# Two layers on one core: the low-rank weights of the second layer leave the experts' loop

## The chip, the cores and the metric

The kernel runs on one core of one Trainium2 chip, as one program. The metric is the device time of one execution in microseconds; each kernel is executed several times and the median is compared. All tensors are 32-bit floats. The core has five engines that run their own instruction streams and meet at semaphores: TensorE (PE), VectorE (DVE), ScalarE (ACT), GpSimd (POOL) and SyncE (SP), which here only issues DMAs. GpSimd issues the gathers (indirect DMAs).

## The reference, cut to what matters

```python
x = hidden_states                                  # 8 x 256 tokens, 512 features
xn = layernorm(x)
x = x + L0_attn(xn) + L0_ffn(xn)                   # linear attention, 32 heads; 16 experts, 2 chosen, and a shared one
xn = layernorm(x)
x = x + L1_attn(xn) + L1_ffn(xn)                   # one head of 128; low-rank experts

def L1_ffn(xf):                                    # K 64, TOPK 16, RANK 16
    scores = xf @ Wr.T
    top_vals, top_idx = top_k(scores, 16)
    gates = softmax(top_vals)                      # scattered into G: tokens x 64
    h = einsum('nd,krd->nkr', xf, A)               # A: 64 x 16 x 512
    out = einsum('nkr,kdr->nd', h * G[:, :, None], B)
    return out * 2.0
```

## The kernel before, in words

Every product of 32-bit floats is made in three passes of TensorE (`three_passes`, L98 to L105). For that an operand is split into a high part, a cast to TensorE's rounded format, and a low part, the rest. The cast is ScalarE's, the subtraction VectorE's or GpSimd's. So a weight costs a load, a cast ("high") and a subtraction ("low") before it can be used.

The program has three stages. The first is layer zero's attention and shared expert, some 2000 us long. The second is the routed experts, `routed_experts` (L2219): 31 tiles of 256 slots, each with one expert's weights. The third is layer one, `layer_one` (L2536): four groups of 512 tokens.

**The experts' loop.** For each tile SyncE loads the expert's weights (L2320, L2325) and stores the result (L2355). GpSimd copies two columns of slot numbers (L2493), gathers 256 rows of 512 in two indirect DMAs into `exin` (L2498), and splits the third weight (L2527). TensorE transposes the rows (L2378), multiplies by the first two weights (L2393) and by the third. Rows are gathered four tiles ahead, into two buffers: the gather of tile i + 4 waits until the transposes of tile i + 2 are done. The steps are rolled into hardware loops (`all_steps`, L2265), two tiles per round.

Into these steps layer one's own weights are fitted in pieces, for they don't depend on anything. `w1h` and `w1l` hold them side by side as columns: the projections, the router and the output weight first (L_A = 2304 columns), then A (4096 columns, from L_A to L_B), then B (4096 columns, from L_B). A and the first part are loaded, cast and subtracted in 28 pieces, one a tile. The first 16 are 256 columns of A each, which are also brought into another order by the split: 128 rank positions of a part, "a rank's part" from here on, are made contiguous. They are read with a stride of 8 elements. The other 12 pieces are 192 contiguous columns of the first part. The piece is loaded by L2332, cast by L2440 and subtracted by L2521, which stands in GpSimd's queue between the copy of the slot numbers and the gathers. After 16 pieces the rolled loop is left and a second one begins, since the pieces are of another kind.

**The start of layer one.** A group's 512 tokens are four tiles of 128. GpSimd waits for the last store of the experts, then gathers for each tile the rows of both choices from `y_slots` (L3004; the first choice's land in `l_stage`, the second's in `l_p` and `l_pt`). VectorE adds them, weighted, to `acc` (L2865), takes the statistics (L2875 to L2881), and needs a square root of ScalarE (L2796). Then it normalises (L2888), and TensorE transposes two tiles (L2747) and starts the projections. The second two tiles follow. The order of all work in layer one is the list `events` (L2607 to L2634), which each engine walks for its own part. In the first group it is: statistics and transposes of two tiles, projections of the first half (`part` 0 to 2), the same for the second half, `score`, `part` 3 and 4, `scores_t` (the router), `part` 5, `route`, `vt`, `score`, the first `hid` (the product with rank 0 of A), then `top` (the 16 largest of 64 scores and the gates, all on VectorE, L2921 to L2949), `probs`, `attend`, `gates`. After that `mix` and `hid` of the ranks follow, and every `mix` but the first uses a part of B.

B isn't in the experts' loop. SyncE issues its first four parts (8 DMAs of 128 KB, L3043) as soon as the experts' last store is issued, and the other four once the rows of the first group are gathered (L3040). ScalarE casts the first four at the very start, before any event (L2788), and the others after each `mix` (L2827). GpSimd subtracts the first four after the gathers of the first group (L3020) and the others at L3033. Between them GpSimd gathers the next group's rows of the first choice (after the first group's last transposes, L3001), adds the output bias to the four tiles of `acc` (L3027; once both halves are normalised) and gathers the second choice's rows (after `attend`, L2999).

## Time and profile before

| | us |
|---|---|
| median of 3 executions | 2498.89 |
| lowest, highest | 2497.11, 2499.97 |
| the profiled execution, its own time | 2500.58 |
| its span in the profile | 2498.70 |
| TensorE busy in it | 2436.5 (98%) |
| VectorE, ScalarE, GpSimd busy | 1577.9, 1347.7, 1592.7 |
| of the span: experts' loop, first to last transposes of the rows in question | 2036.72 to 2188.42 |
| TensorE's pause after the experts | to 2221.38 |

The profile is of one execution; its times are microseconds from the start of its span. What moves an instruction's start is read from the idle time in square brackets behind its row, with the engine or transfer that ended it. Where several rows of the same kind follow each other without a gap, they stand as one with a count. Names in the rows are the program's, without the digits: `l_wh` and `l_wl` are the high and low weights of layer one, `l_raw` and `l_w_late` the loaded pieces and B, `exin` the gathered rows.

### The profile page before, as it was taken

Reading aid. Unit: us, or ns where it says so; the run is one execution under the profiler, and the core shown is the slowest. Engines: PE = TensorE matmul, PEld = TensorE weight load, DVE = VectorE, ACT = ScalarE, POOL = GpSimd, SP = SyncE. Lnnn points to the kernel's source line nnn. Section 1 sums busy time; section 2 is a strip of 40 time slices with the busy share of each in tenths; the row PEclk is TensorE's granted clock in tenths of the full one; section 3 lists DMA queues with packets and bytes.
Section 4 is the critical chain, followed back from the end, with each engine's and each line's share of the span. In section 5 each row is a group of like instructions: output and inputs, shape, how many; then the busy total and the mean of one; then the engine's idle time right before and its main releaser. Section 6 shows DMA issues by size and latency. Waiting matters only on the chain.

```text
span 2498.7 us, 42232 instructions
## 1 busy us (share of the span) xinstructions
PE 2436.5 (98%) x13818; PEld 2115.3 (85%) x13818; DVE 1577.9 (63%) x2437; ACT 1347.7 (54%) x2668; POOL 1592.7 (64%) x1529
## 2 busy tenths in 40 slices
PE   7999999999999999999999999999999999969999
PEld 6888888898989898788988888888888878857887
DVE  6565565657574747886565565657575788965554
ACT  5556555655555555555555565555565558733221
POOL 5666767676676764767677767777776678842210
PEclk9999999999999999999999999999999999989999
DMA  4210111111111112311121111111111178941110
GB/s 159 88 55 31 63 46 47 55 46 53 40 55 45 52 43 85 106 56 50 36 63 40 52 55 39 54 46 55 38 59 43 32 249 301 307 139 34 51 34 34
DMA packets 89454, 183.36 MB, mean 73 GB/s; under 512 B 12626, under 2 KB 38882, under 8 KB 89366
## 3 DMA queue, kind: packets, MB, share of 16 engines
q1 hardware_dynamic: 80822, 165.41, 20.2%
q0 software_dynamic: 8544, 16.82, 2.2%
q8 instruction: 50, 0.82, 0.1%
q14 instruction: 38, 0.31, 0.0%
HBM read 163.28 MB, written 26.79 MB: 76 GB/s over the span
## 4 chain that ended last, share of the span: by engine, by line
PE 86%; DVE 5%; POOL 3%; issue 2%; DMA 2%; ACT 1%; SPq 0%; POOLq 0%; DVEq 0%; ACTq 0%
PE bank L102 27%; PE bank L103 26%; PE bank L104 26%; PE bank L1117 2%; PE bank L1144 2%; DMA exin<-xn_rows,ecur 1%; POOL exin L2498 1%; POOL el L2527 1%; DVE acc L2899 1%; POOL wl L2039 0%; PE bank L2378 0%; POOL l_wl L2521 0%; PE bank L2747 0%; PE bank L2758 0%; PE bank L574 0%
## 5 line engine op out<-in xcount | busy, mean ns | idle before, releaser
L2039 POOL TENSOR_TENSOR wl<-w_in,wh 128x512 fp32r<-128x512 f32 x510 | 621.9, 1246 | 304.5 <-ACT wh L1443 301.6
L102 PE MATMUL bank<-xh,wh 128*128 128x512 f32 x1400 | 556.9, 398 | 0.6 <-DVE bank L1750 0.6
L104 PE MATMUL bank<-xh,wl 128*128 128x512 f32 x1400 | 545.7, 390 | 0.0
L103 PE MATMUL bank<-xl_sums,wh 128*128 128x512 f32 x800 | 312.4, 390 | 0.0
L104 PEld LDWEIGHTS bank<-xh,wl 128*128 128x128 f32 x1400 | 262.8, 188 | 56.7
L102 PEld LDWEIGHTS bank<-xh,wh 128*128 128x128 f32 x1400 | 263.5, 188 | 52.8 <-DVE bank L1750 4.2
L2057 POOL TENSOR_TENSOR sqacc<-sqacc,sq 128x512 f32<-128x512 f32 x128 | 173.2, 1353 | 198.7 <-ACT sq L1428 194.1
L1443 ACT CAST wh<-w_in 128x512 fp32r<-128x512 f32 x502 | 261.9, 567 | 32.2 <-POOL w_in L533 32.2
L102 PE MATMUL bank<-wh,xh 128*128 128x256 f32 x912 | 259.1, 284 | 0.1
L103 PE MATMUL bank<-wl,xh 128*128 128x256 f32 x912 | 258.3, 283 | 0.0
L1787 DVE TENSOR_TENSOR acc<-bank,acc 128x512 f32<-128x512 f32 x240 | 162.3, 686 | 118.6 <-PE bank L104 116.5
L103 PE MATMUL bank<-xl,wh 128*128 128x512 f32 x600 | 234.1, 390 | 0.0
L1428 ACT ACTIVATE sq<-bank 128x512 f32<-128x512 f32 x128 | 76.6, 599 | 267.9 <-DVE yf L1762 267.9
L1762 DVE SCALAR_TENSOR_TENSOR yf<-gT,bank 128x512 f32<-128x512 f32 x128 | 87.9, 687 | 194.4 <-PE bank L1144 194.1
L102 PE MATMUL bank<-oh,yh 128*128 128x512 f32 x512 | 202.1, 395 | 2.0 <-DVE yl L1767 1.1
L103 PE MATMUL bank<-ol,yh 128*128 128x512 f32 x512 | 199.7, 390 | 0.0
L104 PE MATMUL bank<-oh,yl 128*128 128x512 f32 x512 | 199.3, 389 | 0.0
L1750 DVE TENSOR_TENSOR bank<-bank,t 128x512 f32<-128x512 f32 x128 | 88.7, 693 | 167.7 <-PE bank L104 167.2
L1767 DVE SCALAR_TENSOR_TENSOR yl<-yf,little,yh 128x512 fp32r<-128x512 f32 x128 | 155.1, 1212 | 61.0 <-ACT yh L1433 58.3
L102 PEld LDWEIGHTS bank<-wh,xh 128*128 128x128 f32 x912 | 175.4, 192 | 1.8 <-DVE xl L585 0.9
L103 PEld LDWEIGHTS bank<-wl,xh 128*128 128x128 f32 x912 | 175.3, 192 | 0.7
L103 PEld LDWEIGHTS bank<-xl_sums,wh 128*128 128x128 f32 x800 | 150.6, 188 | 25.4
(380 smaller groups left out, 6365.7 us busy)
## 6 DMA issues: line engine op xcount, KB each, us to landing
w_in<-in_w_pairs_dram SPq DMA_DIRECT2D x100, 512.0 KB, 3.8
o_in<-in_o_pairs_dram SPq DMA_DIRECT2D x32, 512.0 KB, 3.5
eraw<-in_ex_dram SPq DMA_DIRECT2D x31, 513.0 KB
y_slots<-ey SPq DMA_DIRECT2D x30, 512.0 KB
w_in<-in_w_pairs_dram SPq DMA_DIRECT2D x56, 256.0 KB, 3.0
dcur<-in_decay_dram SPq DMA_DIRECT2D x32, 256.0 KB
eraw<-in_ex_dram SPq DMA_DIRECT2D x31, 256.0 KB
out_dram<-acc SPq DMA_DIRECT2D x16, 256.0 KB, 2.0
```

What stands on the lines that cost most here:

```text
L102: pe.matmul(out, wh, mh, start=start and i == 0, stop=False, skip_group_check=True)
L103: pe.matmul(out, wh, ml, start=False, stop=False, skip_group_check=True)
L104: ins = pe.matmul(out, wl, mh, start=False, stop=stop and i == n - 1, skip_group_check=True)
L1117: ins = pe.matmul(sc[1][:, to * P:(to + 1) * P], kT[:, hd, c], qT[:, hd, c], start=True, stop=True)
L1428: a.activation(sq[:], ot[:], ACT.Square).then_inc(a_sq, 1)
L1443: a.copy(wh[:, cols], w_in[:, cols]).then_inc(w_hi, 1)
L1750: v.tensor_tensor(pj[2][:], pj[1][:], t5[:], ALU.add).then_inc(v_c, 1)
L1762: v.scalar_tensor_tensor(yf[:], gT[:, g % 2, t * GT:(t + 1) * GT], 1.0, ot[:], ALU.add, ALU.mult).then_inc(v_y, 1)
L1767: v.scalar_tensor_tensor(yl[g % 2][:], yf[:], nwcur[:, g % 2:g % 2 + 1], yh[g % 2][:].bitcast(F32), ALU.mult, ALU.subtract).then_inc(v_yl, 1)
L1787: v.tensor_tensor(now[:, t, :], op[t % 2][:], now[:, t, :], ALU.add).then_inc(v_acc, 1)
L2039: pool.tensor_tensor(wl[:, cols], w_in[:, cols], wh[:, cols].bitcast(F32), ALU.subtract).then_inc(w_lo, 1)
L2057: pool.tensor_tensor(sqacc[:, c], sqacc[:, c], sq[:], ALU.add).then_inc(p_sq, 1)
```

## The change

Both A and B are now loaded and split at the start of layer one.

- In the experts' loop only the 12 pieces of 192 columns are left, in the first 12 steps. The rolled loop is left after 6 rounds instead of 8, and the second loop has no pieces at all. Where GpSimd has no piece, it does a subtraction of one column on `rest_of_wait` instead, ahead of the gathers, which takes over the waits.
- SyncE loads A in four DMAs of 512 KB into `raw_a`, which lies where the second buffers of `x1h` and `x1l` are (first used in the second group). They wait for the second choice's rows of tile 1, the fourth gather. B follows in eight DMAs of 256 KB, after the eighth gather.
- A is split by rank: eight casts of 128x4x128 and eight subtractions, read with a stride of 8 elements as the pieces were. ScalarE does the casts at fixed places in the events: three after the second transposes' cast, three before `score` 0, two and the first of B before `scores_t`, two of B before `score` 1, one before `attend`; the last four after each `mix`, as before. ScalarE no longer casts B ahead of all events.
- GpSimd subtracts three parts of A after the first eight gathers, and then, behind the next group's gathers and ahead of the output bias, five of A and three of B; the last five of B behind the second choice's gathers.
- TensorE waits for the low part of rank i before `hid` i of the first group; ScalarE waits for the last low part of A before it writes over `raw_a` in the second group.

```diff
-PIECE_A, PIECE = 2 * P, 192
-PIECES_A = NR * SEC // PIECE_A
-PIECES = PIECES_A + L_A // PIECE
+PIECES = 12
+PIECE = L_A // PIECES
...
             for b in range(2):
-                run(r, b, True)
+                run(r, b)
...
-            all_steps(sp, run, PIECES_A // 2 - 1)
+            all_steps(sp, run, PIECES // 2 - 1)
...
-            is_piece, k, half_k, nk = tile(r, b, -1, PIECES)
-            if is_piece:
-                (high, low), raw = split_parts(k, half_k, nk, a_first)
+            is_piece, k, _, nk = tile(r, b, -1, PIECES)
+            if is_piece and pieces:
+                c = bass.ds(k * PIECE, PIECE)
                 pool.wait_ge(a_l1, k + 1)
-                pool.tensor_tensor(low, raw, high.bitcast(F32), ALU.subtract).then_inc(lo_l1, 1)
+                pool.tensor_tensor(w1l[:, c], l1raw[nk][:], w1h[:, c].bitcast(F32), ALU.subtract).then_inc(lo_l1, 1)
+            elif is_tile:
+                pool.tensor_tensor(rest_of_wait[:], ident[:, 0:1], ident[:, 0:1], ALU.subtract)
             if is_tile:
                 gather(n)
...
+    HIGHS = [("a", 0), ("a", 1), ("a", 2), ("a", 3), ("a", 4), ("a", 5), ("a", 6), ("a", 7)] + [("b", i) for i in range(NR)]
+    LOWS = HIGHS
+
+    def late_parts(what, i):
+
+        if what == "a":
+            return raw_rank[:, i], [w[:, i] for w in split_rank]
+        cols = slice(L_B + i * D, L_B + (i + 1) * D)
+        return w1_late[:, i * D:(i + 1) * D], [w[:, cols] for w in (w1h, w1l)]
...
+    late_casts = {("score", 0, 0): HIGHS[3:6], ("scores_t", 0, 0): HIGHS[6:9], ("score", 0, 1): HIGHS[9:11],
+                  ("attend", 0, 0): HIGHS[11:12]}
...
             if g == 0:
-                pe.wait_ge(lo_late, PIECES + i + 1)
+                pe.wait_ge(lo_late, late_n(LOWS, "b", i))
...
                 bank = fill(hb, h_fill, h_taken, (what, g, i))
+                if g == 0:
+                    pe.wait_ge(lo_late, late_n(LOWS, "a", i))
...
-        for k in range(EARLY):
-            late_high(k)
+        def late_high(*parts):
+            for part in parts:
+                raw, (high, _) = late_parts(*part)
+                if part == HIGHS[0]:
+                    a.wait_ge(dma_late, 16 * ((PIECES + 1) // 2 + KC))
+                if part == ("b", 0):
+                    a.wait_ge(dma_b, 16 * NR)
+                a.copy(high, raw).then_inc(a_late, 1)
+
         for what, g, i in events:
+            late_high(*late_casts.get((what, g, i), ()))
...
             if what == "xt":
+                if (g, i) == (1, 0):
+                    a.wait_ge(lo_late, late_n(LOWS, "a", NR - 1))
                 a.copy(*x_part(xh, g, i, bank)).then_inc(q["a_xh"], 1)
+                if (g, i) == (0, 1):
+                    late_high(*HIGHS[0:3])
...
-        late_low(*range(EARLY))
+        late_low(*LOWS[0:3])
         gather(1, 0)
+        late_low(*LOWS[3:11])
         pool.wait_ge(dma_bo, 16)
...
             if g == 0:
-                late_low(*range(EARLY, NR))
+                late_low(*LOWS[11:])
...
+        sp.wait_ge(dma_y[1][1], 16)
+        for k in range(KC):
+            c = slice(2 * k * SEC, 2 * (k + 1) * SEC)
+            sp.dma_start(raw_a[:, c], l1_w[:, L_A + c.start:L_A + c.stop]).then_inc(dma_late, 16)
+        sp.wait_ge(dma_y[1][TPG - 1], 16)
         for k in range(NR):
-            if k == EARLY:
-                sp.wait_ge(dma_y[1][TPG - 1], 16)
-            for j in range(2):
-                to = w1_late[j:P:2, k * D:(k + 1) * D]
-                sp.dma_start(to, by_gate[NR * j + k]).then_inc(dma_late if k < EARLY else dma_rest, 16)
-
+            sp.dma_start(w1_late[:, k * D:(k + 1) * D], by_gate[k]).then_inc(dma_b, 16)
```

How the instructions stand in a row is best seen at three places. The first is GpSimd's queue in the second rolled loop of the experts, one tile; before:

```order
L2493 ISA [waits token_table_in,e_dma_x0]
L2493 COPY ecur_79<-token_at 128x2
L2494 REGISTER_ALU
L2516 REGISTER_ALU [waits e_p_cur]
L2520 ISA [waits e_pe_xt]
L2521 ISA [waits e_a_l1]
L2521 TENSOR_TENSOR l_wl<-l_raw_87,l_wh 128x192
L2498 DMA exin_75<-xn_rows,ecur_79 128x512 x2
L2526 ISA
L2527 TENSOR_TENSOR el_83<-eraw_74,eh_69 128x512 [waits e_a_hi3]
```

The same tile with the change:

```order
L2472 ISA [waits token_table_in,e_dma_x0]
L2472 COPY ecur_79<-token_at 128x2
L2473 REGISTER_ALU
L2495 REGISTER_ALU [waits e_p_cur]
L2502 TENSOR_TENSOR e_rest_of_wait<-ident 128x1 [waits e_pe_xt]
L2477 DMA exin_75<-xn_rows,ecur_79 128x512 x2
L2507 ISA
L2508 TENSOR_TENSOR el_83<-eraw_74,eh_69 128x512 [waits e_a_hi3]
```

The subtraction of 192 columns and its wait for ScalarE (`e_a_l1`) are gone, and one column stands in their place.

The second place is ScalarE's queue at the start of layer one, before (`e_dma_l10` is the semaphore on which the late loads count):

```order
L2786 CAST l_wh<-l_w_late 128x512 [waits e_dma_l10]
L2786 CAST l_wh<-l_w_late 128x512 x3
L2796 ACT_TABLE_LOAD
L2796 ACTIVATE l_root<-l_var 128x2 [waits l1_v_var]
L2841 CAST x1h_103<-bank 128x2x256 [waits l1_pe_m] x2
L2812 ACTIVATE l_qkv<-bank,l_bq 128x256 [waits l1_pe_h,l1_dma_c]
L2796 ACTIVATE l_root<-l_var 128x2 [waits l1_v_var]
```

and with the change:

```order
L2798 ACT_TABLE_LOAD
L2798 ACTIVATE l_root<-l_var 128x2 [waits l1_v_var]
L2845 CAST x1h_104<-bank 128x2x256 [waits l1_pe_m] x2
L2789 CAST l_wh<-l_raw_a 128x4x128 [waits e_dma_l10]
L2789 CAST l_wh<-l_raw_a 128x4x128 x2
L2814 ACTIVATE l_qkv<-bank,l_bq 128x256 [waits l1_pe_h,l1_dma_c]
L2798 ACTIVATE l_root<-l_var 128x2 [waits l1_v_var]
```

The wait for the late loads has moved from ahead of the first square root to ahead of the first projection's copy and the second root.

The third place is GpSimd's queue behind the first group's eight gathers, before:

```order
L3012 TENSOR_TENSOR l_wl<-l_w_late,l_wh 128x512 [waits e_a_l1] x4
L3004 DMA l_stage<-y_slots,slot_of 128x512 [waits l1_pe_m]
L3004 DMA l_stage<-y_slots,slot_of 128x512 x3
L3027 TENSOR_TENSOR acc<-acc,l_bo 128x512 [waits l1_v_xn,l1_dma_bo]
L3027 TENSOR_TENSOR acc<-acc,l_bo 128x512 x3
L3004 DMA l_p<-y_slots,slot_of 128x512 [waits l1_pe_m]
```

and with the change:

```order
L3018 TENSOR_TENSOR l_wl<-l_raw_a,l_wh 128x4x128 [waits e_a_l1] x3
L3010 DMA l_stage<-y_slots,slot_of 128x512 [waits l1_pe_m]
L3010 DMA l_stage<-y_slots,slot_of 128x512 x3
L3018 TENSOR_TENSOR l_wl<-l_raw_a,l_wh 128x4x128 [waits e_a_l1] x5
L3018 TENSOR_TENSOR l_wl<-l_w_late,l_wh 128x512 [waits e_a_l1] x3
L3033 TENSOR_TENSOR acc<-acc,l_bo 128x512 [waits l1_v_xn,l1_dma_bo]
L3033 TENSOR_TENSOR acc<-acc,l_bo 128x512 x3
L3010 DMA l_p<-y_slots,slot_of 128x512 [waits l1_pe_m]
```

Eight subtractions now stand between the next group's gathers and the additions of the output bias.

## Rows read from the trace of the kernel before

**Rows 1.** Stretches: start:end, us, busy and instructions by engine, TensorE clock, DMA share, GB/s.
```profile
2060.00:2190.00 130.00, 123.87 (x894) 114.46 (x893) 111.82 (x164) 102.82 (x233) 108.51 (x116) 0.99 0.90 305
2200.00:2300.00 100.00, 71.38 (x357) 57.51 (x356) 57.76 (x125) 29.43 (x59) 40.28 (x36) 0.88 0.28 87
2300.00:2498.70 198.70, 195.32 (x899) 159.35 (x898) 101.16 (x262) 49.49 (x100) 23.32 (x20) 1.00 0.11 38
```

**Rows 2.** Timeline, TensorE in the loop: start, us, engine, line, tiles [idle before <-releaser].
```profile
2036.72 1.04 PE L2378 MATMUL bank<-ident,exin 128*128 128x128 f32 x8
...
2073.73 1.41 PE L2378 MATMUL bank<-ident,exin 128*128 128x128 f32 x8 [2.07 <-DMA exin<-xn_rows,ecur]
...
2107.58 1.03 PE L2378 MATMUL bank<-ident,exin 128*128 128x128 f32 x8
...
2112.72 1.03 PE L2378 MATMUL bank<-ident,exin 128*128 128x128 f32 x8
...
2188.42 1.03 PE L2378 MATMUL bank<-ident,exin 128*128 128x128 f32 x8
```

**Rows 3.** Timeline, GpSimd in the loop: second gathers of a tile.
```profile
2037.89 1.00 POOL L2498 DMA_INDIRECT exin<-xn_rows,ecur  x1 [0.30 <-issue]
...
2106.38 1.09 POOL L2498 DMA_INDIRECT exin<-xn_rows,ecur  x1 [0.30 <-issue]
...
2133.24 1.06 POOL L2498 DMA_INDIRECT exin<-xn_rows,ecur  x1 [0.30 <-issue]
...
2138.41 1.36 POOL L2498 DMA_INDIRECT exin<-xn_rows,ecur  x1 [0.30 <-issue]
...
2143.88 1.38 POOL L2498 DMA_INDIRECT exin<-xn_rows,ecur  x1 [0.30 <-issue]
```

**Rows 4.** Timeline, TensorE at the start of layer one.
```profile
2221.38 1.97 PE L2747 MATMUL bank<-ident,l_stage 128*128 128x128 f32 x8 [20.89 <-DVE l_stage L2888]
...
2230.50 1.07 PE L2747 MATMUL bank<-ident,l_stage 128*128 128x128 f32 x8 [0.26 <-DVE l_stage L2888]
...
2252.09 0.63 PE L2763 MATMUL bank<-ident,l_g 128*128 128x128 f32 x4 [0.44 <-DVE l_g L2948]
```

**Rows 5.** Groups by form, GpSimd: line, operation, tiles, form xcount | busy, mean ns | idle before.
```profile
L2521 POOL TENSOR_TENSOR l_wl<-l_raw,l_wh 128x256 f32 x14 | 13.6, 972 | 6.0 <-POOL ecur L2493 4.8 <-PE bank L2378 1.2
...
L2521 POOL TENSOR_TENSOR l_wl<-l_raw,l_wh 128x192 f32 x8 | 4.8, 602 | 2.9 <-POOL ecur L2493 2.9
...
L3012 POOL TENSOR_TENSOR l_wl<-l_w_late,l_wh 128x512 fp32r<-128x512 f32 x8 | 10.1, 1275 | 16.9 <-ACT l_wh L2786 15.6 <-issue 1.3
```

**Rows 6.** Groups by form, ScalarE.
```profile
L2440 ACT CAST l_wh<-l_raw 128x256 f32 x14 | 9.9, 710 | 1.1 <-DMA l_raw<-in_l_w_dram 1.1
```

**Rows 7.** Timeline, GpSimd at the start of layer one.
```profile
2207.30 0.95 POOL L3004 DMA_INDIRECT l_p<-y_slots,slot_of  x1 [0.30 <-issue]
...
2214.94 4.92 POOL L3012 TENSOR_TENSOR l_wl<-l_w_late,l_wh 128x512 fp32r<-128x512 f32 x4 [1.28 <-issue]
...
2236.55 5.01 POOL L3027 TENSOR_TENSOR acc<-acc,l_bo 128x512 f32<-128x512 f32 x4
```

**Rows 8.** Timeline, VectorE at the start of layer one.
```profile
2213.88 0.75 DVE L2865 SCALAR_TENSOR_TENSOR acc<-l_p,gate_of,acc 128x512 f32<-128x512 f32 x1 [0.44 <-DMA l_p<-y_slots,slot_of]
...
2215.67 0.56 DVE L2881 TENSOR_SCALAR l_var<-l_mv 128x2 f32<-128x2 f32 x1
...
2218.70 1.19 DVE L93 TENSOR_TENSOR l_root<-l_root,l_rstd 128x2 f32<-128x2 f32 x1
...
2227.84 0.17 DVE L2881 TENSOR_SCALAR l_var<-l_mv 128x2 f32<-128x2 f32 x1
...
2235.88 5.85 DVE L2983 TENSOR_SCALAR l_p<-l_p,l_sum 128x256 f32<-128x256 f32 x1
...
2246.32 0.60 DVE L2923 MAX8 l_top<-l_sr 128x8 f32<-128x64 f32 x4
```

**Rows 9.** Transfers: tile, queue, kind xcount, KB each, median us to landing.
```profile
l_pt<-y_slots,slot_of POOLq DMA_INDIRECT x8, 3.8
```

**Rows 10.** Timeline, ScalarE at the start of layer one.
```profile
2226.92 0.47 ACT L2812 ACTIVATE l_qkv<-bank,l_bq 128x256 f32<-128x256 f32 x1 [2.96 <-PE bank L104]
```

More of the change, by code:

```diff
@@ L2337, in lead, with run @@
             load3(0, 0)
-        def run(r, b, a_first=True):
+        def run(r, b, pieces=True):
             is_tile, i, _, n = tile(r, b, 4)
@@ L2406, in outputs, with run @@
                              True).then_inc(pe_o, 1)
-        def run(r, b, a_first=True):
+        def run(r, b, pieces=True):
             if not isinstance(r, int) or r >= 0:
@@ L2417, in scalar, with run @@
     def scalar(a):
-        def run(r, b, a_first=True):
+        def run(r, b, pieces=True):
             is_tile, i, half, n = tile(r, b, 2)
@@ L2451, in run @@
                 a.copy(yb[n][:, 0, :], op[0][:]).then_inc(a_y, 1)
[L2453 removed]
+        return lambda: run(-1, 0), lambda: all_steps(a, run, PIECES // 2)
     def vector(v):
@@ L2466, in weights_low, with run @@
                                 ALU.subtract).then_inc(v_lo, 1)
-        def run(r, b, a_first=True):
+        def run(r, b, pieces=True):
             is_tile, i, half, n = tile(r, b, 2)
@@ L2509, in lead, with run @@
                 gather(b)
-        def run(r, b, a_first=True):
+        def run(r, b, pieces=True):
             is_tile, i, half, n = tile(r, b, 4)
```

72 lines of the change are left out of this document (26 added, 46 removed).

## The prediction, made before the change was run

> **What bounds the kernel now.** I read the stretches first. After the experts' loop, from 2300 us to the end, TensorE is busy 195.32 of 198.70 us, so whatever moves the start of that part moves the end one for one. From 2200 to 2300 it is busy only 71.38 of 100, and in the experts' loop 123.87 of 130 [rows 1]. So there are two places to win or lose: the loop, and the start of layer one.
>
> In the loop TensorE begins a tile with eight transposes of gathered rows. Undisturbed, the next tile follows 5.14 us later (2107.58, 2112.72). From 2036.72 to 2188.42 there are 27 periods, which would be 27 x 5.14 = 138.8 us at that pace; they took 151.7. So 12.9 us are lost, mostly in waits for gathered rows such as the 2.07 us before 2073.73 [rows 2]. The gathers come from GpSimd's queue. Its second gather of a tile starts at 2037.89 and, twelve tiles later, at 2106.38: 5.71 us a tile. There the tile's piece of the weight of layer one is 256 columns wide. With pieces of 192 columns two neighbours are 5.17 us apart (2133.24, 2138.41), but then 5.47 (2138.41, 2143.88), and the second gather itself takes 1.36 to 1.38 us instead of 1.06 [rows 3]. GpSimd never stands still for anyone in these rows, so its queue is what sets the loop, 5.2 to 5.7 against TensorE's 5.14. DMA is the next bound: busy share 0.90 at 305 GB/s [rows 1].
>
> At the start of layer one TensorE stands still for 20.89 us, to 2221.38, and then waits again briefly before 2230.50 and before 2252.09, each time for VectorE [rows 4].
>
> **The loop, part by part.** Removed: 16 pieces of 256 columns (A, read with a stride of 8 elements), at 972 ns each on GpSimd and 710 ns on ScalarE, and 16 x 128 KB of loads. Moved forward: the 12 pieces of 192 columns, 602 ns on GpSimd [rows 5, 6]. Added on GpSimd, in steps with no piece: one subtraction on 128x1, of which no row exists; it lies between nothing and the 0.60 us of the 192 columns that it stands in for, and one column is nearest to nothing: I take 0.1.
> Step 1, tiles with a piece (12): 0.972 - 0.602 = 0.37 us less each, so 5.71 becomes 5.34 and TensorE reaches the twelfth tile 12 x 0.37 = 4.4 us earlier. If GpSimd runs at its free 5.17, it is 6.5 us; if it falls into the 5.47 of the later rows, 2.9.
> Step 2, tiles without (14 periods, 2112.72 to 2188.42, 5.41 each [rows 2]): GpSimd's 5.17 less 0.60 plus 0.1 is 4.7 us (5.0 with the long gather), below TensorE's 5.14. Then TensorE is the bound, and 14 x (5.41 - 5.14) = 3.7 us go. Nothing is won if GpSimd and VectorE stay locked at 5.47; see rival B.
> DMA: the loads of A were 2.1 MB in about 24 tiles. At the measured 0.90 for 305 GB/s, 339 GB/s is full; a tile moves 305 x 5.4 = 1.65 MB, and at 5.14 us that would be 320 GB/s with the pieces, near 0.92 of full with the smaller ones and less without. So it stays as loaded as it was, and I charge nothing for it.
> Sum of the loop: **8 us won**, 2.9 to 10.2.
>
> **The start of layer one.** Before, eight loads of B stood ahead of the first gathers, and ScalarE had to wait for them and cast them before its square root. Now nothing is loaded until the gathered rows of two tiles are there.
> Step 3: the fourth gather is issued at 2207.30 and VectorE gets its rows only at 2213.88, 6.6 us later. The median landing of such a gather is 3.8 us, so 2211.1 is possible: 2.8 us won [rows 7, 8, 9]. From there VectorE reached its variance 1.79 us later (2215.67). From the variance to TensorE's transposes it took 5.71 us the first time, with GpSimd's splits beside it and the casts ahead of the root. The second time, with GpSimd idle, it took 2230.50 - 2227.84 = 2.66 [rows 4, 8]. So TensorE starts at 2211.1 + 1.8 + 2.7 = 2215.6, **5.8 us earlier**.
> Step 4, most of it is given back. The 2 MB of A are issued at about 2211.3, behind the same two tiles, and share the DMA with four gathers (0.5 to 1 MB): 2.6 to 3.1 MB at 305 to 339 GB/s is 8 to 10 us, so A is there at 2219.5 to 2222. ScalarE's first cast waits for all of it, and behind that cast are queued three casts, the copy of the first projection and the second root. Strided casts cost 2 x 710 = 1.42 us at most, and 1.1 if only the slope counts: about 3.3 us for three. The projection's copy was at 2226.92, 5.5 us after TensorE's start [rows 10]; now, instead of 2221.1, it comes at about 2221 + 3.3 = 2224.4. The root follows at 2224.8, and the norm's chain has GpSimd's first three splits of A beside it, as the first chain had before: 2.7 plus 1 is 3.7 us from the root's place on. The second transposes start at about 2228.6 instead of 2230.50: **1.9 us won**, from 5 won (A there in time) to 1 lost (A at 2224).
> Step 5: before the copy of the router's scores ScalarE now casts two parts of A and one of B, 2.8 us, of which about 0.9 is not covered by TensorE's work there. **0.9 lost**, 0 to 1.5.
> Step 6: GpSimd in the first group. It gets eight strided splits more. One costs between 1.66 us (slope of the two widths) and 2 x 972 = 1.94; I take 1.8. After the transposes, at 2229.7, come four gathers of 1.25 us (to 2234.7), five splits of A (to 2243.7), three of B at 1.275 (to 2247.5) [rows 5], and then the four additions of the output bias (5.01 us, to 2252.5). Before, those ran from 2236.55 to 2241.56, beside a VectorE instruction that took 5.85 us [rows 7, 8]. It was hidden, since TensorE had projections to do. Now they fall on the top-16 and gate chain, for which TensorE waits (before 2252.09, by 0.44 us [rows 4]). Without them the gates would come at 2252.1 - 1.9 + 0.9 = 2251.1. The last scaling of the gates can't pass the additions, so it ends no earlier than 2253.4, and with a delay or two by splits about 2254.5: **3.4 lost**, 0.5 to 7.
>
> The rule that speaks for a milder case: the Trainium skill, SBUF — State Buffer, "Who interferes with whom", says that whoever issues first holds the shared pair of ports for its instruction and the other blocks fully. Read so, VectorE should get in after one addition. The trace agrees for the splits, each of which waits on a semaphore: VectorE's 1.19 us at 2218.70 ends at one of their boundaries. It does not for the four additions in a row: 5.85 us [rows 7, 8]. By the rule alone step 6 would cost about 1 us instead of 3.4, and the sum would be 8 won and not 5.6.
>
> **Sum.** 8 + 1.9 - 0.9 - 3.4 = 5.6 us won. The profiled execution took 2500.58 us (span 2498.70), so 2495.0; the median shown is 1.7 lower, 2498.89, so **2493.3**. A measurement of this kernel can tell about 0.2%, 5 us, from no change; the forecast lies just past that.
>
> **Rivals.**
> A. *The tail keeps its gain* (A lands before ScalarE asks, additions block little): loop 8, tail 3 or more: 11 to 14 won, about 2486. For it: the 1.19 us delays; against: 8 to 10 us of transfers have only 7 us of cover, from 2211.3 to 2218.2, where ScalarE is free (before, 2.6 us after TensorE's start: it idled 2.96 us up to 2226.92 [rows 10]).
> B. *GpSimd isn't relieved.* The second gather grew to 1.38 us just when the piece shrank, so that the period stayed at 5.47, as if something else held it. If the lock holds with no piece at all, the loop wins only 3 us, and with the tail's 2.4 lost the time is within 1 us of before, 2498. Against it: 5.17 was there once with a piece, and without one the gather comes 0.5 us earlier, to another point of VectorE's work [rows 3].
> C. *Slower: VectorE is shut out in the first group.* If a tensor_scalar (the scaling of the second probabilities, ready at about 2244) finds no gap in GpSimd's unbroken row of splits and additions, it waits until 2252.5; the maxima, replacements and gates behind it took 5.8 us (2246.32 to 2252.09 [rows 4, 8]), so the gates come at about 2258.9, 6.8 us later than before, and A at 2224 adds 3. With 8 won in the loop that is still only 2 us slower. It decides for slower by over 5 us where the loop wins 4 or less: then 2504. For it: the 5.85 us; against: the splits' own boundaries.
> D. *DMA sets the loop*: the gathers land later as loads bunch. At 0.95 share a tile costs 5.3 us, the loop wins 4: 2497.
>
> **How the numbers follow.** Forecast (4 to 8 us won) 0.43; A 0.18; B 0.13; D 0.11; C 0.15 (two thirds of it slower by over 5 us, a third about the same). Faster by over 0.2% (below 2493.9): 0.18 of A, 0.3 of the forecast, together with a little of B, 0.50. Within 0.2%: 0.37. Slower: 0.13. The range 2486 to 2502 leaves out about 0.1 on either side.
>
> **What would show it.** Right: periods near 5.14 in the second half of the loop, no wait for gathered rows there; the last transposes of an expert at about 2180; TensorE's pause after the loop near 15 to 17 us instead of 20.89; then ScalarE waiting for the load of A, and a VectorE tensor_scalar of several us beside the additions, now in front of the gates. Wrong: second gathers of 1.4 us and periods of 5.4 without a piece (B); no wait of ScalarE on A (A); gates more than 6 us after where the start would put them (C).

## The result and the profile after

Over 22 executions each, on the same chips, the changed kernel takes 2505.24 us (median) and the kernel before 2500.72. The ratio is 1.0015, 95% interval 1.0009 to 1.0021: by it the change is **about 3.8 us slower, where 5.6 us faster was forecast** (the two medians are 4.5 us apart). The profiled execution has a span of 2502.0 us, against 2498.70.

Up to the second transposes of layer one nearly everything came as forecast. The windows of the changed kernel answer to [rows 1]: in the loop TensorE is now busy 129.15 of 130 us, but from 2200 to 2300 only 72.81 of 100, with its clock at 0.85 on average (0.88 before).

```profile
2060.00:2190.00 130.00, 129.15 (x947) 120.32 (x945) 104.44 (x173) 100.58 (x229) 96.68 (x114) 1.00 0.87 290
2200.00:2300.00 100.00, 72.81 (x337) 59.12 (x338) 66.80 (x120) 34.94 (x63) 48.18 (x39) 0.85 0.27 88
```

The first and the last transposes of the same 27 periods in the loop (timeline of TensorE, as in [rows 2]):

```profile
2034.68 1.03 PE L2358 MATMUL bank<-ident,exin 128*128 128x128 f32 x8
...
2173.24 1.03 PE L2358 MATMUL bank<-ident,exin 128*128 128x128 f32 x8
2178.38 1.03 PE L2358 MATMUL bank<-ident,exin 128*128 128x128 f32 x8
```

That is 143.70 us instead of 151.70, so 8.0 us won. Then TensorE at the start of layer one, to be held against [rows 4]:

```profile
2205.34 1.97 PE L2749 MATMUL bank<-ident,l_stage 128*128 128x128 f32 x8 [15.09 <-DVE l_stage L2894]
2207.86 0.58 PE L100 MATMUL bank<-x1h,l_wh 128*128 128x256 f32 x1 [0.55 <-DVE x1l L2995]
2214.73 0.39 PE L100 MATMUL bank<-x1h,l_wh 128*128 128x256 f32 x1 [1.38 <-ACT l_qkv L2814]
2218.55 1.06 PE L2749 MATMUL bank<-ident,l_stage 128*128 128x128 f32 x8 [2.12 <-DVE l_stage L2894]
...
2242.06 2.07 PE L2760 MATMUL bank<-l_qkv 128*128 128x256 f32 x4 [10.44 <-DVE l_sr L2979]
```

From the last transposes of an expert to the first of layer one it is 26.96 us instead of 32.96. At 2205.34 the kernel is 16.0 us ahead (2.0 of them from layer 0, which also differs between executions), at the second transposes 11.95. The matmuls of the second scores stood at 2242.37 before; now they start at 2242.06. **Between 2218 and 2242 the whole lead is gone**, in one wait of 10.44 us for VectorE's copy of the router's scores. VectorE and GpSimd in that stretch:

```profile
2224.59 0.17 DVE L2987 RECIPROCAL l_sum<-l_sum 128x2 f32<-128x2 f32 x1 [1.09 <-ACT l_p L2836]
2224.79 16.88 DVE L2989 TENSOR_SCALAR l_p<-l_p,l_sum 128x256 f32<-128x256 f32 x2
2241.60 0.41 DVE L2979 COPY l_sr<-bank 128x256 f32<-128x256 f32 x1
...
2224.61 8.11 POOL L3018 TENSOR_TENSOR l_wl<-l_raw_a,l_wh 128x512 fp32r<-128x512 f32 x5
2232.69 3.69 POOL L3018 TENSOR_TENSOR l_wl<-l_w_late,l_wh 128x512 fp32r<-128x512 f32 x3
2236.35 4.90 POOL L3033 TENSOR_TENSOR acc<-acc,l_bo 128x512 f32<-128x512 f32 x4
```

The first scaling of the probabilities is ready 0.18 us after GpSimd began a row of twelve instructions, and ends 0.4 us after the last of them, at 2241.25. It is the instruction that took 5.85 us in [rows 8]. The copy of the scores is queued behind it. The pause also lowers TensorE's clock; the second fence has the same stretches of the kernel before:

```profile
2235.00:2245.00 10.00, 2.94 (x7) 2.39 (x8) 7.73 (x5) 0.00 (x0) 6.26 (x6) 0.50 0.00 0
2245.00:2250.00 5.00, 5.00 (x21) 4.06 (x21) 3.77 (x29) 2.87 (x10) 0.00 (x0) 0.70 0.00 0
```

```profile
2235.00:2245.00 10.00, 9.34 (x57) 7.36 (x56) 7.47 (x6) 3.58 (x11) 6.25 (x6) 1.00 0.25 74
2245.00:2250.00 5.00, 5.00 (x28) 4.17 (x27) 4.20 (x30) 2.58 (x10) 0.00 (x0) 1.00 0.00 0
```

At 0.50 (1.2 GHz) up to 2245 and 0.70 on average up to 2250, TensorE's next products take longer: the one that stood at 2253.05 starts at 2255.51. From 0.3 us ahead it is 2.5 us behind, and 3.3 at the end.

### The profile page after: what moved, and what is told of

It reads as the page before. It is cut to its first block, busy times and chain, and to the rows that moved or that the text cites. A ratio compares the mean times of both kernels' runs of the same rounds, so it can differ in the third digit from the quotient of the medians.

```text
span 2502.0 us, 42151 instructions
## 1 busy us (share of the span) xinstructions
PE 2438.2 (97%) x13818; PEld 2118.5 (85%) x13818; DVE 1574.5 (63%) x2437; ACT 1346.9 (54%) x2660; POOL 1593.2 (64%) x1538
## 4 chain that ended last, share of the span: by engine, by line
PE 90%; DVE 5%; DMA 2%; issue 1%; POOL 1%; ACT 1%; SPq 0%; POOLq 0%; DVEq 0%; ACTq 0%
PE bank L100 28%; PE bank L101 28%; PE bank L102 28%; PE bank L1115 2%; PE bank L1142 2%; DMA exin<-xn_rows,ecur 1%; PE bank L2358 1%; DVE l_p L2989 1%; DVE acc L2905 1%; PE bank L2760 0%; DMA l_raw_a<-in_l_w_dram 0%; POOL acc L2181 0%; PE bank L572 0%; DVE xl L583 0%; PE bank L2777 0%
```

## Experiments

All variants were timed in five rounds beside the kernel before on the same chip; ratios are to that. Where a variant is given in us against the kernel before, it is by the ratio; two variants are compared by their medians, and ran on one chip.

**Is it the shut-out, or ScalarE's casts?** The kernel before with eight subtractions of 128x512 ahead of the four additions in GpSimd's queue. They write to the second buffers of `x1h` and `x1l`, so ScalarE's first cast of the second group waits for them; nothing else is changed (the code is shortened):

```
+        for k in range(8):
+            pool.wait_ge(a_late, PIECES + 1)
+            pool.tensor_tensor((xh, xl)[k // 4][1][:, k % 4, :], ..., ALU.subtract).then_inc(extra, 1)
```

> The kernel before, with eight more GpSimd subtractions of 128x512 (about 10 us, each behind a wait that is already met, results unused) between the next group's gathers and the additions of the output bias; nothing else is moved, no load, no cast. Theory 1 (a VectorE tensor_scalar finds no gap in an unbroken row of GpSimd instructions): the scaling of the first probabilities grows from 5.85 us to 15 to 17 us, TensorE waits about 10 us for it before the second scores, and the time is 8 to 11 us longer (+0.3 to +0.45%). Theory 2 (the changed kernel's loss is ScalarE's: the wait for A and the casts ahead of its copies and exponentials; the long scaling is as harmless as it was before): within 1 us of before.

Measured: 1.0033 [1.0023, 1.0044], 8.3 us slower. VectorE, GpSimd and TensorE in it:

```profile
2239.42 14.02 DVE L2986 TENSOR_SCALAR l_p<-l_p,l_sum 128x256 f32<-128x256 f32 x2
2240.12 4.03 POOL L3027 TENSOR_TENSOR x1h<-l_wh 128x512 fp32r<-128x512 f32 x4
2244.12 4.03 POOL L3027 TENSOR_TENSOR x1l<-l_wh 128x512 fp32r<-128x512 f32 x4
2248.11 4.91 POOL L3034 TENSOR_TENSOR acc<-acc,l_bo 128x512 f32<-128x512 f32 x4
...
2253.83 2.08 PE L2759 MATMUL bank<-l_qkv 128*128 128x256 f32 x4 [8.31 <-DVE l_sr L2976]
```

A longer row on GpSimd alone makes the same picture, without the change's casts, loads or strided reads.

**Does the row do harm later too?** The changed kernel, the row held back until the first probabilities are scaled:

```
+        pool.wait_ge(q["v_prob"], 1)
         late_low(*LOWS[3:11])
```

> The changed kernel, with one wait more: GpSimd starts the eight splits (five of A, three of B) only when the first probabilities are scaled. Theory 1: the 16.3 us scaling becomes 0.3 to 0.6 us, but the second scaling, ready some 9 us later, is now shut out until the additions end, about 7 us; the gates come about 5 us earlier than in the changed kernel, so 3 to 6 us less than that and at or just below before (-0.1%). Theory 2: nothing is won, or up to 1 us lost.

Measured: 1.0012 [1.0003, 1.0022]. The hoped-for gain did not come, and by its time alone this run would fit theory 2 as well; the trace decides. The first scaling takes 0.62 us, but a later instruction that reads and writes only SBUF is caught, a tensor_scalar on two columns (theory 1 had named the second scaling), and TensorE waits 8.25 us for what follows from it:

```profile
2233.63 0.62 DVE L2989 TENSOR_SCALAR l_p<-l_p,l_sum 128x256 f32<-128x256 f32 x2
...
2242.49 8.57 DVE L2985 TENSOR_SCALAR l_mx<-l_mx 128x2 f32<-128x2 f32 x1
...
2246.11 4.92 POOL L3034 TENSOR_TENSOR acc<-acc,l_bo 128x512 f32<-128x512 f32 x4
```

It ends at 2251.06, GpSimd's row at 2251.03. So what is left of GpSimd's row decides, not the size of what is shut out.

**Is it this form of instruction?** The scaling written as a tensor_tensor with a broadcast factor, in both kernels:

```
-                    ins = v.tensor_scalar(pr[...], pr[...], sm[...], None, ALU.mult)
+                    ins = v.tensor_tensor(pr[...], pr[...], sm[...].to_broadcast([P, S]), ALU.mult)
```

> The changed kernel, with the scaling of the probabilities as a tensor_tensor with the sum's reciprocal broadcast over 256 columns instead of a tensor_scalar (same values). Theory 1, in the form that only the tensor_scalar of a whole row is shut out while a tensor_tensor gets in at the end of the running GpSimd instruction: each of the two takes up to 1.9 us instead of 16.3 for the first; TensorE's 10.44 us wait before the second scores goes, the time is 7 to 11 us below the changed kernel and 3 to 7 below before (-0.15 to -0.3%). If every VectorE instruction that reads only SBUF is shut out, it stays as it was. Theory 2: it stays as it was.

> The kernel before, with the same tensor_tensor for the scaling. Theory 1: the 5.85 us become at most 2.6 for both, but TensorE had work beside them, so the time stays within 1 us of before. Theory 2: the same. It tells whether the form by itself is worth anything.

Measured: after_tt 1.0032 [1.0023, 1.0041], with the scaling at 16.94 us; before_tt 0.9998 [0.9989, 1.0007], with 5.99 us, where 2.6 or less was expected of it if the form mattered. Both forms are shut out alike.

**Why does VectorE not get in between two of GpSimd's instructions?** Each of the splits waits on a semaphore, and in the row of twelve that let nobody in. In the next variant, from the fifth late split on, each split and addition waits for the *end* of the one before it:

```
                 pool.wait_ge(a_late, late_n(HIGHS, *part))
+                if LOWS.index(part) > 3:
+                    pool.wait_ge(lo_late, late_n(LOWS, *part) - 1)
...
+                if t == 0:
+                    pool.wait_ge(lo_late, late_n(LOWS, "b", 2))
+                elif t < TPG:
+                    pool.wait_ge(q["p_bo"], t)
```

> The changed kernel once more, beside the next three. Both theories: 1.001 to 1.002 of before. Theory L (the loop has two rhythms, 5.14 us a tile, or 5.34 to 5.46, and an execution falls into one of them by chance): its single executions spread over some 8 us or more, wider than those of before. Theory S (the rhythm belongs to the kernel's edit): the spread is like that of before, and the profiled loop has 143 to 144 us for its last 27 periods again.

> The changed kernel, but from its fifth late split on each split and each of the first group's four additions waits until the one before it has ended. Theory G (VectorE is shut out because GpSimd's next instruction is already waiting at its engine when one ends; a real gap lets VectorE in): the first scaling of the probabilities takes 4 us or less instead of 16.88, TensorE's wait for VectorE's copy of the scores (10.44) falls below 3, and the kernel is 7 to 11 us faster than the unchained one, 0.997 to 0.999 of before. Theory N (GpSimd keeps the ports whatever the gap, or VectorE's long instruction needs more than one gap): the scaling still takes over 10 us, the time stays at 1.001 or goes up by the gaps, 11 x 0.1 to 0.2 us.

> The kernel before with the eight added subtractions of the earlier run (whose row with the four additions made the scaling take 14.02 us, +8.3 us in all), now each waiting for the end of the one before, the additions too. Theory G: the scaling falls to 4 us or less, TensorE's wait of 8.31 us for the copy of the scores to under 2, and the time to within 2 us of before (0.9995 to 1.0010). Theory N: 1.003 again, scaling over 10 us.

Measured on one chip: the changed kernel again 2510.42 us, 1.0025 [1.0014, 1.0036]; with gaps 2502.41, 0.9995 [0.9986, 1.0004], **8.0 us less**; before_load with gaps 1.0008 [0.9999, 1.0017] instead of 1.0033. In after_chain the scaling beside the same row of splits:

```profile
2234.53 2.08 DVE L2989 TENSOR_SCALAR l_p<-l_p,l_sum 128x256 f32<-128x256 f32 x2
2234.52 9.11 POOL L3020 TENSOR_TENSOR l_wl<-l_raw_a,l_wh 128x512 fp32r<-128x512 f32 x5
...
2248.07 5.46 POOL L3039 TENSOR_TENSOR acc<-acc,l_bo 128x512 f32<-128x512 f32 x4 [0.17 <-POOL l_wl L3020]
```

Eleven waits make the row of twelve 2.4 us longer (19.0 us for 16.6), and no tensor instruction of VectorE up to the gates is held past the end of the GpSimd instruction that it met. So a real gap lets VectorE in: that part of theory G is shown. The ratio 0.997 to 0.999 expected with it was too low, and the changed kernel itself came out above its 1.001 to 1.002.

Theory G's reason, that VectorE is shut out wherever the next instruction is already waiting, isn't shown, and the traces speak against it as a general rule: in other rows without gaps VectorE did get in at the end of one instruction. The first row of three in the changed kernel:

```profile
2212.30 4.65 POOL L3018 TENSOR_TENSOR l_wl<-l_raw_a,l_wh 128x512 fp32r<-128x512 f32 x3 [8.49 <-ACT l_wh L2789]
2212.75 1.12 DVE L2887 TENSOR_SCALAR l_var<-l_mv 128x2 f32<-128x2 f32 x1
```

VectorE is through at 2213.87, the first split at 2213.84, and the second followed at once. In the kernel before, all four casts of B were done at 2216.42, so the waits of the third and the fourth split had been met before the third began (2217.38). Yet VectorE ends at 2218.66, just behind the third split (2218.64), and not with the row (2219.86, [rows 7]):

```profile
2214.24 2.18 ACT L2786 CAST l_wh<-l_w_late 128x512 fp32r<-128x512 f32 x4 [13.81 <-DMA l_w_late<-in_l_w_dram]
2218.24 0.42 DVE L92 TENSOR_TENSOR l_rstd<-l_rstd,l_var 128x2 f32<-128x2 f32 x1
```

What decides whether a row without gaps shuts VectorE out to its end stays open.

**Short rows released by VectorE** in place of gaps, with the second gathers drawn ahead (the splits of B and the additions keep their gaps):

```
+        doses = {("a", 3): ("v_prob", 1), ("a", 5): ("v_r", 1), ("a", 6): ("v_prob", 2)}
...
+                if part in doses:
+                    pool.wait_ge(q[doses[part][0]], doses[part][1])
...
-        late_low(*LOWS[3:11])
+        late_low(*LOWS[3:8])
+        gather(1, 1)
+        late_low(*LOWS[8:11])
...
```

> The changed kernel with GpSimd's late splits in short rows, each released by VectorE: two of A behind the first scaled probabilities, one behind the copy of the scores, two behind the second scaled probabilities, the gathers of group 1 next, then three of B and the additions, one behind the end of the other. Both theories of the shut-out have the first scaling short. If rows of at most two splits (3.2 us) are all that VectorE can meet: no VectorE instruction over 4 us from the first probabilities to the gates, gates 8 us or more earlier than in the changed kernel, total 0.9955 to 0.998 of before. If the lead is used up elsewhere (GpSimd too late for group 1, or TensorE's lower clock): 0.999 to 1.001, with TensorE waiting for a split of A or for the gathered rows of group 1.

Measured: 1.0004 [0.9995, 1.0013]. The gates are early (TensorE takes them at 2250.39 with a wait of 0.80), but the lead is used up behind them: in the first group's later products TensorE waits 2.02 us for one of the late splits and, at 2274.86, 6.03 us for VectorE, for which it waited 3.06 in the kernel before. The time is that of the second outcome; of the waits named with it, only the one for a split came (of B, not of A).

**What does the load of A cost (step 4)?** On top of the gaps, ScalarE's casts of A leave the place ahead of the first projection's copy and the second root:

```
-    late_casts = {("score", 0, 0): HIGHS[3:6], ("scores_t", 0, 0): HIGHS[6:9], ("score", 0, 1): HIGHS[9:11],
-                  ("attend", 0, 0): HIGHS[11:12]}
+    late_casts = {("score", 0, 0): HIGHS[0:3], ("scores_t", 0, 0): HIGHS[3:5], ("score", 0, 1): HIGHS[5:7],
+                  ("top", 0, 0): HIGHS[7:9], ("attend", 0, 0): HIGHS[9:10], ("gates", 0, 0): HIGHS[10:12]}
...
-                if (g, i) == (0, 1):
-                    late_high(*HIGHS[0:3])
```

> The changed kernel with the waits that make gaps (0.9995 of before), and ScalarE's casts of A no longer ahead of the first projection's copy and the second root: the first three stand behind the casts of the second transposes, the rest in smaller lots up to the gates. Theory P (what step 4 put at 4.1 us is ScalarE standing at the load of A with the copy and the root behind it, and that pause lets TensorE's clock fall to 0.5 a second time): the second transposes come 9 to 10 us after the first instead of 13.69, the granted clock is 1.00 from 2230 on, the matmuls of the first scores take 1.1 us and not 2.07, TensorE's gates transposes 5 to 7 us nearer to its start, total 0.9970 to 0.9985 of before. Theory Q (the time is owed to something else, such as GpSimd's splits on VectorE's norm): the second transposes still 12 us or more after the first, total unchanged at 0.9995.

Measured: 0.9981 [0.9972, 0.9990], on another chip than gaps alone. So both were run once more beside each other, with the moved casts without gaps:

> The changed kernel with gaps once more, so that the next three stand beside it on one chip. 0.9985 to 0.9998 of before; a loop of 144 or of 148 to 149 us for its last 27 periods.

> Gaps, and ScalarE's casts of A moved, once more. Theory P (the pause at the load of A costs 4 us in itself and, by the second fall of TensorE's clock, 2 to 3 more): 4 to 7 us faster than the run with gaps alone beside it. Theory Q (its 0.9981 against 0.9995 was the chip and the loop's rhythm): within 2 us of it.

> The casts of A moved as in the run beside it, but without the waits that make gaps. If the two losses are separate: the second transposes come 10 us after the first, but one VectorE instruction of the first group (a scaling or the small one on the maxima) again takes 8 us or more beside GpSimd's row of five splits, three splits and four additions, and the time is 5 to 9 us above the run with gaps: 1.0000 to 1.0015 of before. If the other places of the casts alone break GpSimd's row (each split then follows its cast closely): no instruction over 5 us, 0.998 to 0.999.

Measured on one chip: gaps alone 2497.57 us, 0.9988 [0.9979, 0.9997]; gaps and moved casts 2495.60, 0.9978 [0.9969, 0.9987]; moved casts without gaps 2502.10, 1.0005 [0.9995, 1.0014]. TensorE's timeline from its start on, first with gaps alone, then with moved casts too, and the window from 2220 to 2225 of each in the same order:

```profile
2206.83 1.97 PE L2749 MATMUL bank<-ident,l_stage 128*128 128x128 f32 x8 [15.27 <-DVE l_stage L2894]
2220.14 1.06 PE L2749 MATMUL bank<-ident,l_stage 128*128 128x128 f32 x8 [2.07 <-DVE l_stage L2894]
2246.01 1.08 PE L2765 MATMUL bank<-ident,l_g 128*128 128x128 f32 x4 [2.25 <-DVE l_g L2954]
```

```profile
2207.39 1.97 PE L2749 MATMUL bank<-ident,l_stage 128*128 128x128 f32 x8 [15.12 <-DVE l_stage L2892]
2217.83 1.07 PE L2749 MATMUL bank<-ident,l_stage 128*128 128x128 f32 x8 [1.72 <-DVE l_stage L2892]
2243.90 0.67 PE L2765 MATMUL bank<-ident,l_g 128*128 128x128 f32 x4 [3.90 <-DVE l_g L2952]
```

```profile
2220.00:2225.00 5.00, 3.89 (x17) 3.33 (x18) 1.98 (x3) 4.17 (x5) 2.85 (x3) 0.71 0.75 234
```

```profile
2220.00:2225.00 5.00, 5.00 (x34) 4.40 (x35) 2.92 (x5) 5.00 (x10) 4.33 (x3) 1.00 0.61 219
```

The second transposes come 10.44 us after the first instead of 13.31, and the clock no longer falls in 2220 to 2225. But 1.65 us more is lost at the gates, and the time is only 2.0 us less, where P expected 4 to 7 and Q up to 2. So P's signs are there at the second transposes, but its size isn't. The first transposes of the second group come 63.4 us after the first ones with gaps alone and 63.7 with moved casts, so these two profiles show nothing left of the lead there. The clock isn't tied to this pause alone either: the first scores take 1.13 us in five of the six profiles with moved casts, where chain2 has 2.08, but also in chain_long_rest below, whose casts stand where they stood. The third run shows that the gaps are needed here too: without them it is 6.5 us slower, with one long instruction again (8 us or more was expected):

```profile
2229.87 5.81 DVE L2983 TENSOR_SCALAR l_mx<-l_mx 128x2 f32<-128x2 f32 x1
...
2229.51 6.14 POOL L3016 TENSOR_TENSOR l_wl<-l_raw_a,l_wh 128x512 fp32r<-128x512 f32 x4
2237.82 1.52 POOL L3016 TENSOR_TENSOR l_wl<-l_raw_a,l_wh 128x512 fp32r<-128x512 f32 x1 [2.16 <-ACT l_wh L2789]
```

VectorE ends at 2235.68; GpSimd's four splits ended at 2235.65, and it then had to wait for ScalarE. In the same execution VectorE and GpSimd later take turns in a row without gaps, the four additions (4.90 us undisturbed):

```profile
2246.84 6.42 POOL L3031 TENSOR_TENSOR acc<-acc,l_bo 128x512 f32<-128x512 f32 x4
2248.64 5.83 DVE L2903 SCALAR_TENSOR_TENSOR acc<-l_stage,gate_of,acc 128x512 f32<-128x512 f32 x4
```

**Other places for the load, the loop and the gates.** All with gaps. A loaded without waiting for the gathered rows:

```
-        sp.wait_ge(dma_y[1][1], 16)
         for k in range(KC):
             c = slice(2 * k * SEC, 2 * (k + 1) * SEC)
```

> The changed kernel with gaps, and the loads of A issued right behind the last loads of the loop, without waiting for the gathered rows of two tiles. If the load's late landing is what costs at the start (P): ScalarE's wait of 3.73 us for A is gone, the second transposes 9 to 11 us after the first; against that the first gathered rows share the DMA with 2 MB and TensorE starts layer one 0 to 5 us later than 15.1 us after its last matmul. Net between 4 us faster and 2 slower than with gaps alone: 0.998 to 1.0003. If A doesn't matter (Q): no gain, only the later start, 1.000 to 1.0015.

The kernel before with gaps between its four additions:

```
+                if 0 < t < TPG:
+                    pool.wait_ge(q["p_bo"], t)
```

> The kernel before, its first group's four additions of the output bias each waiting for the end of the one before. The scaling of the first probabilities falls from 5.85 us to 3 or less, but TensorE had projections to do meanwhile and waited for the copy of the scores by only 0.39 us: 0.9995 to 1.0003, both theories of the shut-out alike. If it came out 2 us or more faster, the four additions would have cost the kernel before something that the trace doesn't show.

The loop's small subtraction made wider:

```
-                pool.tensor_tensor(rest_of_wait[:], ident[:, 0:1], ident[:, 0:1], ALU.subtract)
+                pool.tensor_tensor(rest_of_wait[:], ident[:, 0:1].to_broadcast([P, PIECE]), ..., ALU.subtract)
```

> The changed kernel with gaps, the small subtraction of the loop (128x1) made as wide as a piece (128x192, about 0.6 us) in all tiles without a piece. Theory L (the loop has two rhythms, and which one it falls into depends on when GpSimd's third split meets VectorE's two; in the slow one GpSimd comes early): GpSimd is 0.4 us later and the loop settles at 5.14 us a tile, 143 to 146 us for its last 27 periods instead of 147 to 149, and the time is 2 to 5 us less than with gaps alone. Theory W (what counts is GpSimd's work per tile): periods of 5.4 to 5.5, 150 us or more, 2 to 4 us slower than with gaps alone.

The early load, the wider subtraction and the moved casts together:

> All that helped together: gaps, casts of A moved, A loaded without waiting for the gathered rows, the loop's small subtraction as wide as a piece. If the gains add up: loop 144 us in most executions, TensorE's pause after the loop up to 2 us longer, A split early; 0.9965 to 0.9978 of before. If the early load brings nothing once the casts are moved (nobody waits for A then) and its longer pause counts: 0.9978 to 0.9985, no better than the moved casts with gaps.

Moved casts, and GpSimd silent until the gates are there. The second choice's gathers are drawn ahead, and the first split of B stands before the last three of A:

```
-    LOWS = HIGHS
+    LOWS = HIGHS[0:5] + [("b", 0)] + HIGHS[5:8] + HIGHS[9:]
...
+        late_low(*LOWS[3:5])
         gather(1, 0)
-        late_low(*LOWS[3:11])
+        pool.wait_ge(q["v_g"], 1)
+        gather(1, 1)
+        late_low(*LOWS[5:11])
...
```

> Gaps and moved casts (0.9978 to 0.9981 of before), and GpSimd silent while VectorE works on the top-16 and the gates: two more splits of A stand ahead of the first gathers of group 1, then GpSimd waits for the gates, issues the second gathers and only then the first split of B, the other splits and the additions, with gaps. In the run with moved casts the pieces of the gates chain took 3.4 us more than alone (l_left 1.35 for 0.43, l_gates 1.37 for 0.42, l_g 2.12 for 0.88, others the rest) and TensorE waited 3.9 us for it. If GpSimd's place beside that chain is the cost: the wait falls to 1 us or less and the time by 2 to 3 us, 0.9965 to 0.9972. If its work costs wherever it stands (group 1's combinations and hidden parts then meet it): the gates are early, but the transposes of group 1 are not, 0.9978 to 0.9990.

And moved casts once more, beside it:

> Gaps and moved casts a third time, beside the silent version on one chip: 0.9975 to 0.9985 of before.

| variant | us | ratio, interval |
|---|---|---|
| chain_early_load (A loaded early) | 2497.61 | 0.9987 [0.9978, 0.9996] |
| before_chain (kernel before, gaps) | 2500.98 | 1.0002 [0.9993, 1.0011] |
| chain_long_rest (wider subtraction) | 2497.90 | 0.9991 [0.9982, 1.0000] |
| late_early_rest (all together) | 2498.83 | 0.9993 [0.9984, 1.0002] |
| quiet_gates (GpSimd silent) | 2497.02 | 0.9985 [0.9976, 0.9994] |
| chain_late_a3 (moved casts) | 2496.15 | 0.9985 [0.9976, 0.9994] |

With the early load ScalarE no longer waits for A, but TensorE pauses 17.26 us after the loop instead of 15.1; neither it nor the wider subtraction can be told from gaps alone (0.9988 and 0.9995), and the two together with moved casts are 3.2 us slower than the moved casts alone, on one chip. The longer pause (17.28 for 15.12) is 2.2 us of that; the rest is open. before_chain came as both theories said: the 5.85 us of the kernel before was hidden. In quiet_gates TensorE waits only 0.39 us at the gates, but the splits that were held back are then waited for themselves, and group 1 waits for VectorE:

```profile
2244.30 0.63 PE L2765 MATMUL bank<-ident,l_g 128*128 128x128 f32 x4 [0.39 <-DVE l_g L2952]
...
2251.14 0.47 PE L100 MATMUL bank<-l_wh,l_hh 128*128 128x512 f32 x1 [2.78 <-POOL l_wl L3018]
2259.02 0.47 PE L100 MATMUL bank<-l_wh,l_hh 128*128 128x512 f32 x1 [2.15 <-POOL l_wl L3018]
...
2274.99 1.94 PE L2749 MATMUL bank<-ident,l_stage 128*128 128x128 f32 x8 [3.26 <-DVE l_stage L2921]
```

So the silence moved the loss and didn't remove it: the time is that of the moved casts beside it (2497.02 and 2496.15).

**The loop's two rhythms.** The length of the last 27 periods, read in each profile: kernels with the loop of before 151.70, 153.86, 155.02, 151.04, 149.67 (mean 152.3); kernels with the loop of the changed one 143.50 to 149.87, mean 146.2 over 13 (the two with the wider subtraction, 144.2 and 143.55, left out). Seven of these end in periods of 5.14 us, six in periods of 5.34. First the changed kernel, then the same kernel again:

```profile
2124.71 1.29 DVE L2444 TENSOR_TENSOR el<-eraw,eh 128x512 fp32r<-128x512 f32 x2
2126.30 1.30 POOL L2508 TENSOR_TENSOR el<-eraw,eh 128x512 fp32r<-128x512 f32 x1
```

```profile
2124.09 1.29 POOL L2508 TENSOR_TENSOR el<-eraw,eh 128x512 fp32r<-128x512 f32 x1 [0.24 <-ACT eh L2409]
2124.65 1.88 DVE L2444 TENSOR_TENSOR el<-eraw,eh 128x512 fp32r<-128x512 f32 x2 [0.33 <-ACT eh L2415]
2125.98 0.19 PEld L100 LDWEIGHTS bank<-exth,eh 128*128 128x128 f32 x1 [0.18 <-DVE el L2444]
```

In the slow rhythm GpSimd's split starts 0.56 us before VectorE's two and delays them by 0.6 us, and TensorE waits 0.18 for them in every tile. Theory L's spread is there: the single times of after_again reach from 2504.05 to 2512.99, though those of before on that chip also reach over 8 us (2498.36 to 2506.56). What puts an execution into one rhythm wasn't found; chain_long_rest doesn't show it, as both others with the changed loop beside it were in the fast one too.

## Why the prediction was wrong

- **Loop, steps 1 and 2: right**, 8.0 us won in the profiled execution as summed (4.3 in the first 13 periods, 3.7 in the other 14). Over all profiles it is 6.1 (152.3 to 146.2), since some fall into the slow rhythm; that is a mild form of rival B, inside the stated 2.9 to 10.2.
- **Step 3: right** in the profiled pair, TensorE 6.0 us nearer to the loop's end (5.8 said). But the profile of the kernel before was the best of five here: from the last transposes of an expert to the first of layer one they have 32.96 to 36.76 us, mean 35.2, and 13 profiles of the changed start 26.94 to 28.40, mean 27.7. Over all it is 7.6.
- **Step 4: right in place and size.** ScalarE waited for A, with the projection's copy and the root behind it; from the first to the second transposes 4.1 us were given back (3.9 said). Not foreseen was the clock, at 0.66 on average from 2220 to 2225, behind that pause. With the casts out of the way the kernel was 2.0 us faster, and the profiles don't show where these 2.0 us come from.
- **Step 5** can't be read apart: the casts stand ahead of the copy of the transposed scores as said, but VectorE, which needs what follows from it, was shut out by then.
- **Step 6 is what failed.** It let the row of splits and additions fall on the gate chain and cost 3.4 us, 7 at most, because VectorE would get in at the splits' boundaries. The prediction's ground was one row of splits in the kernel before, each of which waits on a semaphore. Its example, the 1.19 us at 2218.70, doesn't bear that out, for it ends at 2219.89 with the last split of the row (2219.86); the 0.42 us at 2218.24 does. But what held for that row didn't hold for the new one: its twelve instructions were unbroken for VectorE, and they met the *first* probabilities, which had taken 5.85 us before and looked hidden. With the row three times as long (5.0 us before, 16.6 now) the same wait outgrew its cover. Of the lead 11.6 us went by 2242, and another 2.8 in the products behind it, at the lower clock. Gaps gave 8.0 us back.
- **The rule that was weighed there**, of the Trainium skill, SBUF — State Buffer, "Who interferes with whom", has the ports held for one instruction. The runs show both: VectorE was blocked across twelve instructions (16.88 us), against the rule, and let in after one where each waited for the end of the one before (2.08 us), but also in some rows without gaps (1.12 us at 2212.75). So the rule can't be relied on for a row.
- **Rival C** had this mechanism, with 0.15, but placed it at the second probabilities with 6.8 us, and let it become slower only where the loop won little. The point from which it decides was wrong: it decides as soon as the row covers the copy of the scores, for which TensorE waits.

Once VectorE gets in, the sum holds up to the gates. From the first transposes of layer one to those of the gates it was 30.7 us before, 48.6 with the change, and 40.5 and 39.2 with gaps; the prediction's own times, 2254.5 less 2215.6, give 38.9. The total doesn't reach 5.6 us: with gaps alone it is 1.3 and 3.0 us faster (0.9995, whose interval reaches past 1, and 0.9988). With the casts moved as well it is 0.9978, 0.9981 and 0.9985 of before in three measurements, by these ratios 3.7 to 5.5 us faster, each interval below 1. That version beats both kernels. But it also lacks the loss that step 4 had counted, so that it comes near 5.6 is in part luck.

## What to carry to other kernels

Before work is moved to GpSimd, write down the row of its instructions that will follow each other without a gap, and every VectorE instruction on SBUF that falls within it: each may be held to the row's end, however small. It need not be, and these runs don't show what decides. A wait on a semaphore that was met before is no safeguard; a wait for the end of the preceding instruction was one here, at 0.14 to 0.25 us each. And a blocked instruction that is hidden now is a warning: price it for the longer row, not for the present one.

## What the runs showed of the hardware that was not expected

- VectorE is shut out across back-to-back GpSimd instructions, in tensor_scalar and tensor_tensor alike: 16.88 and 16.94 us over twelve, 14.02 over twelve shorter ones, 8.57 for an instruction on 128x2. Not in every row: it got in behind one instruction in rows of three, four splits and four additions (1.12 us at 2212.75; 0.42 at 2218.24; 5.83 for four beside the additions of 6.42). In after_gap1 a copy and a reduction that read a matmul's bank took their usual 0.42 and 0.69 us in the middle of such a row (2239.93, 2241.76).
- GpSimd's subtraction on 128x512 takes 1.62 us where one input is read with a stride of 8 elements and the other operands are four runs of 128 (8.11 for five), 1.23 where all are contiguous (3.69 for three). For ScalarE's cast it is 1.08 (3.23 for three) against 0.61.
- TensorE's clock fell to 0.50 in the pause of 10.44 us, and came back to 1.00 only after 2245. In chain2 pauses of 1.55 us up to 2216.39 and 2.07 us up to 2220.14 were followed by 0.71 on average over 2220 to 2225.
